# Two rotary sums of each unit in the local-attention layers, on VectorE in place of GpSimd

## The reference, cut to what matters

```python
def rotate_half(x):
    x1, x2 = jnp.split(x, 2, -1)
    return jnp.concatenate([-x2, x1], -1)
...
q = l2norm(q) * qs
k = l2norm(k) * ksc
...
q = q * cos * scale + rotate_half(q) * sin * scale
inv = 1.0 / scale
k = k * cos * inv + rotate_half(k) * sin * inv
out = local_attention(q, k, v)
```

## Time and profile before

| | |
|---|---|
| median of 3 runs | 5180.6 us (5169.62 to 5183.22) |
| profiled execution, its own time | 5172.85 us |
| its span, first to last instruction | 5170.8 us |
| mean granted TensorE clock | 0.913 of full speed |
| busy: PE, VectorE, ScalarE, GpSimd | 3934.8, 4374.4, 3040.4, 2537.9 us |

### The profile page before, as it was taken

The page is one execution under the profiler, slowest core; times in us unless marked ns, Lnnn a source line. Parts: engine busy times, 40 slices in busy tenths (PEclk is TensorE's granted clock), DMA queues, the critical chain, the costliest instruction groups (busy, mean ns, idle before and its releaser), DMA issues. The chain is left out here.

```text
span 5170.8 us, 110439 instructions
## 1 busy us (share of the span) xinstructions
PE 3934.8 (76%) x39280; PEld 2903.7 (56%) x39280; DVE 4374.4 (85%) x7725; ACT 3040.4 (59%) x4888; POOL 2537.9 (49%) x1612
## 2 busy tenths in 40 slices
PE   5777777777777777767858678777787787777787
PEld 4655655656656646625535466466465565565565
DVE  8988989979979979954335399799799899898897
ACT  4765756746747747722413477477476476575575
POOL 5645646636636636611010266366366365464562
PEclk8988999989989989986978899899899998899899
DMA  1000000000000000021030000000000000000000
GB/s 47 8 23 11 7 22 12 8 27 6 7 27 7 8 25 8 8 62 26 2 74 1 33 7 7 26 8 21 13 8 20 14 8 19 15 7 22 12 7 12
DMA packets 30608, 88.57 MB, mean 17 GB/s; under 512 B 7505, under 2 KB 13649, under 8 KB 28369
## 3 DMA queue, kind: packets, MB, share of 16 engines
q1 hardware_dynamic: 29104, 80.95, 5.9%
q10 hardware_dynamic: 1152, 3.15, 0.2%
HBM read 38.72 MB, written 1.05 MB: 8 GB/s over the span
## 5 line engine op out<-in xcount | busy, mean ns | idle before, releaser
L771 POOL TENSOR_TENSOR pool<-pool 128x512 f32<-128x512 f32 x768 | 1069.1, 1413 | 968.3 <-DVE pool L869 968.3
L776 POOL TENSOR_TENSOR pool<-pool 128x1024 f32<-128x1024 f32 x384 | 1072.8, 2794 | 168.0 <-DVE pool L880 147.2
L443 PE MATMUL psum<-squares,pool 128*128 128x128 f32 x3072 | 475.4, 304 | 420.8 <-POOL pool L776 259.9
L443 PEld LDWEIGHTS psum<-squares,pool 128*128 128x128 f32 x3072 | 368.9, 153 | 587.2 <-issue 338.1
L880 DVE TENSOR_TENSOR pool<-pool 128x1024 f32<-128x1024 f32 x384 | 678.6, 1806 | 6.8
L483 PE MATMUL psum<-wqkv_hi,xs_lo 128*128 128x512 f32 x1152 | 522.2, 453 | 200.3 <-DVE pool L849 104.6
L646 ACT COPY pool<-psum 64x512 f32<-64x512 f32 x768 | 447.1, 582 | 367.1 <-PE psum L443 361.7
L474 PE MATMUL psum<-pool 128*64 128x128 f32 x6144 | 560.7, 296 | 116.7 <-ACT pool L661 116.5
L420 PE MATMUL psum<-pool 128*128 128x128 f32 x3072 | 455.4, 309 | 130.2 <-ACT pool L646 129.8
L859 DVE TENSOR_REDUCE pool<-pool 128x16 f32<-128x1024 f32 x384 | 449.9, 1210 | 88.1 <-ACT pool L685 88.0
L420 PEld LDWEIGHTS psum<-pool 128*128 128x128 f32 x3072 | 420.4, 219 | 179.4 <-ACT pool L646 167.8
(11 more groups left out here) (165 smaller groups left out, 8247.6 us busy)
## 6 DMA issues: line engine op xcount, KB each, us to landing
pool<-pool SPq DMA_DIRECT2D x192, 128.0 KB, 2.3
pool<-in_wqkv SPq DMA_DIRECT2D x12, 1536.0 KB, 6.0
k_st<-turn_st SPq DMA_DIRECT2D x8, 1536.0 KB, 21.3
pool<-in_wo SPq DMA_DIRECT2D x12, 512.0 KB, 3.6
pool<-in_w SPq DMA_DIRECT2D x12, 341.0 KB, 3.0
pool<-in_w SPq DMA_DIRECT2D x12, 192.0 KB, 2.9
rotary<-in_rotary SPq DMA_DIRECT2D x2, 1024.0 KB, 5.4
pool<-in_scale SPq DMA_DIRECT2D x12, 128.0 KB, 6.2
```

The source lines that it names most:

```text
L443: last = pe.transpose(bank(7 - p % 2)[:, P * j:P * j + P], rot[:, p // 2, 2 * c:2 * c + 2, :], ident)
L771: last = g.tensor_tensor(rot[:, q, :, hd * r:hd * r + hd], qn[:, q, :, hd * (1 - r):hd * (2 - r)], tab, ALU.mult)
L776: g.tensor_tensor(rot[:, q], rot[:, q], by_cos[:, q], ALU.add).then_inc(rot_ready, 1)
```

## The change: what it does

GpSimd keeps the two sine products for each of queries and keys and no longer waits for the cosine products. VectorE does each sum `rot + by_cos` itself, directly behind the cosine product of the same q, after a wait for that product and one for the sine product. `rot_ready` is now counted by VectorE.

```diff
@@ -94,9 +94,9 @@
-            "vector": [qn_ready, cos_ready, s_taken, block_ready, y_ready, norm_step, soft_step,
+            "vector": [rot_ready, qn_ready, cos_ready, s_taken, block_ready, y_ready, norm_step, soft_step,
                        xc_ready, diag_ready, xn_ready, hid_ready, x_ready, var_step, aff_step],
-            "gpsimd": [lo_ready, w_hi, w_split, sin_ready, rot_ready, turn_ready, k_kept],
+            "gpsimd": [lo_ready, w_hi, w_split, sin_ready, turn_ready, k_kept],
@@ -771,9 +771,6 @@
                                     last.then_inc(sin_ready, 1)
-                                    g.wait_ge(sin_ready, done(U, 2, q))
-                                    g.wait_ge(cos_ready, done(U, 2, q))
-                                    g.tensor_tensor(rot[:, q], rot[:, q], by_cos[:, q], ALU.add).then_inc(rot_ready, 1)
@@ -878,6 +875,9 @@
                                 for q in range(2):
                                     tab = turn[:, bass.ds(t, 1), q, :].broadcast_to([P, HEADS, DH])
                                     v.tensor_tensor(by_cos[:, q], qn[:, q], tab, ALU.mult).then_inc(cos_ready, 1)
+                                    v.wait_ge(cos_ready, done(U, 2, q))
+                                    v.wait_ge(sin_ready, done(U, 2, q))
+                                    v.tensor_tensor(rot[:, q], rot[:, q], by_cos[:, q], ALU.add).then_inc(rot_ready, 1)
```

## The result

The changed kernel takes 5724.09 us (median of four runs, 5712.98 to 5726.77) against 5175.65 us for the kernel before in the same comparison: a ratio of 1.1055, interval 1.1032 to 1.1078. It is slower by 10.6%. The forecast was 5763 us, slower by 11%; the range 5640 to 5845 holds the result. The profiled execution took 5724.13 us, 551.3 more than that of before.

The account below looks back on a forecast made before the run. VectorE's list was taken to bound the kernel. Per layer 14 x 3.24 + 1.1 + 2.0 = 48.5 us, 582 for twelve, on 5172.85 gave 5755; 7.8 for the median made 5763 us, range 5640 to 5845.

Parts of the forecast that it names:

- What bounds: Local layers: VectorE's own list, waits inside instructions included, fills the unit's period of 18.19 us.
- Excluding each other, in turns: VectorE's two-input instructions or small scalar operations and GpSimd's work exclude each other and alternate; about 1.09 us per VectorE product.
- The turns one by one: Steady unit: sines, cosines, copy and sums alternate, score maximum +5.08 us; 1.84 returns from small scalar operations; net +3.24.
- Two signs: Profile after the change: GpSimd busy falls by about 1070 us or somewhat less, VectorE busy grows by about 600.
- Unit 0 to 1: No probabilities on VectorE there: turns cost 5.2 us, 4.14 returns from the small chain, so +1.1 us a layer.
- The tail: Behind unit 15: lateness 5.08 us, 2.2 returns at L815; ends 0 (GpSimd's tables set it) and +2.9; taken +2.0.
- The sum: A layer: 14 x 3.24 + 1.1 + 2.0 = 48.5 us; twelve layers 582 us; global stage untouched.
- faster (sines side by side with VectorE): Rival, 4%: shared access sets the pace, 4730 us; weaker form, sines run beside VectorE, -0.35 us a unit, 5120 us.
- the adds at their own time only: Rival, 6%: second sine pair keeps out of VectorE's way; adds cost 0.34 us a unit net, 5245 us.
- the copy that holds nobody up: Rival, 10%: copy does not delay sum 1, or line 745 and tail cost nothing; 5640 us.
- The worse case: Rival, 10%: every VectorE turn takes its full 1.21 us, semaphores add up to 0.1, tail carries 2.9; 5845 us.

Follow-up runs that it names:

- run 1: Changed kernel with VectorE's sum adding the normalised tensor instead of the sine, which GpSimd writes to its own tile: 5659.98 us, ratio 1.094.
- run 2: Changed kernel with VectorE's sums independent of the sine and GpSimd computing no sine products, only counting them: 5145.77 us, ratio 0.9941.
- run 8: Changed kernel with a unit's cosine products and sums moved behind the next unit's square reductions: 5243.16 us, ratio 1.0136.
- run 3: Changed kernel with GpSimd's copy of the kept keys made to wait for both sums of its unit: 5664.14 us, ratio 1.0945.
- run 10: Sums back on GpSimd, with the first cosine product behind the score subtraction and the second behind the square reductions: 5578.52 us, ratio 1.0785.

## Why the prediction was right

**What bounds.** VectorE's list sets the unit before and after (99% and 98% busy). Shown by the periods.

**Excluding each other, in turns.** Shown: the same adds cost as much but for 64 us with their dependence cut (run 1), and almost all of the 1 us for which each instruction is held up goes when the sines are gone (run 2) or lie elsewhere (run 8). The rule of the Trainium skill, SBUF — State Buffer, "Who interferes with whom", that a VectorE instruction with two SBUF inputs and a GpSimd instruction that reads SBUF exclude each other, stood against the change. It holds here (2.2 to 2.3 us beside the sine halves, 1.2 without). The advice of the Trainium skill, GPSIMD Engine Reference, "Engine selection", to put an elementwise add on VectorE since GpSimd takes about twice as long for two inputs, holds for the price of one add (1.23 against 2.37 us) and says nothing of what is held up by then.

**Where the intervals of a layer begin and end.** The terms of the sum can be read off the first layer and the start of the second: the cosine products of unit 15, the score subtraction of unit 15, and the cosine products of units 0 and 1 of the next layer. In the timeline of the kernel before:

```profile
324.40 3.43 DVE L880 TENSOR_TENSOR pool<-pool 128x1024 f32<-128x1024 f32 x2
...
355.79 1.22 DVE L849 TENSOR_TENSOR pool<-psum,pool 128x1024 f32<-128x1024 f32 x1
...
425.10 3.71 DVE L880 TENSOR_TENSOR pool<-pool 128x1024 f32<-128x1024 f32 x2
...
440.56 3.75 DVE L880 TENSOR_TENSOR pool<-pool 128x1024 f32<-128x1024 f32 x2
```

and in that of the changed kernel:

```profile
369.38 2.30 DVE L877 TENSOR_TENSOR pool<-pool 128x1024 f32<-128x1024 f32 x1
...
401.28 1.23 DVE L846 TENSOR_TENSOR pool<-psum,pool 128x1024 f32<-128x1024 f32 x1
...
470.61 1.46 DVE L877 TENSOR_TENSOR pool<-pool 128x1024 f32<-128x1024 f32 x1
...
486.57 1.51 DVE L877 TENSOR_TENSOR pool<-pool 128x1024 f32<-128x1024 f32 x1
```

**The turns one by one.** Predicted 8.65 us from the first cosine product to the score maximum, measured 8.33 in the unit shown. The sequence is as forecast, the copy in front of the last sum included. Line 145 fell to 0.17. In the mean of the 144 intervals the stretch grew by 8.46 - 3.52 = 4.94 us, not 5.08, and the rest of the unit got 1.80 us shorter, not 1.84. A layer is 45.25 us longer at first (score subtraction to score subtraction, unit 0 to unit 0: 416.10 against 370.84). From the cosine products of unit 1 to those of unit 15 it is 44.2 us for 14 intervals, in this layer and in the mean of all twelve: +3.16 and +3.15 each, not +3.24. Two signs came out otherwise than stated. GpSimd's busy time fell by 558.8 us and not by about 1070: the forecast's own turns lengthen the sine halves and the copy, and it left that out of this sign. VectorE's grew by 465.6 us and not by about 600; 69.0 us of the sums' waiting stand as idle time in front of them, in 54 waits of 1.28 us for a sine half, and so outside the busy time.

**Unit 0 to 1.** Predicted +1.1, measured +0.50 (15.46 before, 470.61 to 486.57 after; +0.51 in the mean of all layers). In the first units sum 0 stood idle for 1.28 us on the sine, as here, instead of being held up inside the instruction:

```profile
473.35 2.25 DVE L880 TENSOR_TENSOR pool<-pool 128x1024 f32<-128x1024 f32 x1 [1.28 <-POOL pool L771]
```

The time to the end of the stretch is what the turns give. What I had left out were the two smaller members of the chain, L154 and L152, which come free too (0.53 and 0.34 us before, 0.19 each after). Relative to its size, this term was the one most off.

**The tail.** Predicted +2.0 between ends 0 and 2.9; measured +0.51 from the last unit's cosine product to the subtraction of unit 15 (31.39 before, 369.38 to 401.28 after). The end of GpSimd's tables is the hinge:

```profile
392.46 4.52 POOL L315 TENSOR_TENSOR pool<-rotary,pool 128x2048 f32<-128x2048 f32 x1
```

It ends 27.6 us behind the cosine product, 28.1 before (0.5 earlier, predicted 1), and VectorE has 1.0 us more left behind it. That is the first layer. In the ten layers behind whose last unit GpSimd makes these tables the term is +0.40 to +1.58, +0.86 in the mean. In layers 6 and 12, the last of each half, it makes none, so there is no hinge, and the forecast had overlooked this. There the term is +4.97 and +3.27, above even the upper end of 2.9: the 2.2 us of L815 come back as forecast, but VectorE now idles for TensorE in front of L148, where it did not in layer 6 before:

```profile
2463.50 0.16 DVE L148 TENSOR_SCALAR pool<-psum 128x4 f32<-128x4 f32 x1 [1.50 <-PE psum L550]
```

The mean of all twelve is +1.40. That it lies so near to 2.0 is in part luck: ten layers stay below it and two lie far above.

**The sum.** The three terms, in the mean of all twelve layers, are 44.2 + 0.5 + 1.4 = 46.1 us, against 48.5: 553 us for twelve layers instead of 582. The rest of the program, feed-forward parts and global stage above all, took about 2 us less than before, which gives the 551.3 us between the profiled executions. Of the 39 us between 5763 and 5724, 31 are this: about 14 in the intervals, 7 between units 0 and 1, 7 in the tail. The other 8 are the 7.8 that the forecast added because the median of the runs before lay above the profiled execution; in the changed kernel the two are the same. In the steady units no wait took over elsewhere: the scores kept their slack, and the rotated units came early for nobody. The rivals fall: faster (sines side by side with VectorE) by the four durations; the adds at their own time only by run 2, where even without a sine the unit is 18.32 us, no shorter than before; the copy that holds nobody up by run 3. The worse case, at 5845, did not come either, though run 2 shows that a sum costs more than a released instruction once no sine covers its waits.

**What stays open.** How much of the 64 us of run 1 belongs to the cut dependence and how much to the later start of GpSimd's pair: the two came in one run. Moving ScalarE's squares in run 8 was not tried.

## What to carry to other kernels

Where two engines exclude each other, price an instruction moved between them by what it uncovers, not by its own duration alone: here two adds cost 2.7 us a unit by themselves and the work left on GpSimd, which slid under VectorE's two-input instructions, another 3.4, against 3.0 that came back elsewhere. Lay what cannot run together beside what can (reductions, instructions out of PSUM, transposes) and then decide the allocation: the same move lost 548 us in one order and won 498 in another. Hold-ups hide inside busy time; compare the duration of one instruction shape in different places before believing a busy share. And where two engines take turns, 0.1 us in a start can decide who goes first.

## What the runs showed of the hardware that was not expected

The turns are strict in the units read: an instruction that waits goes ahead when the other engine's current one ends, even where the other has its next ready (1.08 to 1.09 us behind it for a VectorE product or sum). Size does not matter: a 32-element scalar operation of 0.18 us took 1.77 beside a 2.37 us sum, and in run 10 such an operation took 1.91. The block transposes (434 ns in the mean of every run) and the reductions of the squares (1.21 or 1.22 us in the mean of every run) never waited. Having waited has a small return: a GpSimd sine half released by VectorE takes 1.16 to 1.2 us, and 1.3 when it starts free.
